# A macaron block on one core: products that clamp, a half-angle arc tangent, norms moved from Pool to ACT, a new order of the mixer, and an earlier routing of the first block

## The reference

```
x = x + 0.5 * moe(layernorm(x))          # "call 0"
x = x + attn(layernorm(x))               # the mixer
x = x + 0.5 * moe(layernorm(x))          # "call 1", the same weights

moe:   shared = (silu(x@sw1) * (x@sw2)) @ sw3
       probs = softmax(x@rw + rb); top 2 of 8 experts, weights renormalised
       routed = sum over the two of w * ((silu(x@ew1[e]) * (x@ew2[e])) @ ew3[e])     # hidden 256

attn:  z, xBC, dt_raw = split(rmsnorm(x) @ in_proj)         # 256, 256+16+16, 4
       u, B, C = split(silu(conv4(xBC))); B = B/(|B|+eps); C = C/(|C|+eps)
       dt = softplus(dt_raw + dt_bias); A = exp(A_log)      # A: 4 heads x 16 states
       step t:  S = 1/(1 + dt^2 A)
                w = S*(w - dt*A*y + dt*B*u);  y = y + dt*w;  o = y . C
       h = x + ((o + D*u) * silu(z)) @ out_proj
       out = h + (silu(rmsnorm(h)@gate) * (rmsnorm(h)@up)) @ down      # hidden 352
```

## Time and profile before

| what | us |
|---|---|
| median of 3 runs | 932.72 (928.23 to 933.27) |
| the profiled execution's own time | 924.96 |
| its span | 923.2 |
| call 0, routing and shared expert | 0 to 131.8 |
| call 0, expert tiles and answers | 131.8 to 275.7 |
| the mixer | 275.7 to 640.8 |
| call 1, routing and shared expert | 640.8 to 764 |
| call 1, expert tiles, then the last combines | 764 to 923.2 |

### The profile page before, as it was taken

The page is one execution under the profiler, slowest core; times in us unless marked ns, Lnnn a source line. Parts: engine busy times, 40 slices in busy tenths (PEclk is TensorE's granted clock), DMA queues, the critical chain, the costliest instruction groups (busy, mean ns, idle before and its releaser), DMA issues. The chain is left out here.

```text
span 923.2 us, 13673 instructions
## 1 busy us (share of the span) xinstructions
PE 666.9 (72%) x3736; PEld 480.5 (52%) x3736; DVE 580.0 (63%) x1762; ACT 351.0 (38%) x592; POOL 597.5 (65%) x744
## 2 busy tenths in 40 slices
PE   2636769899834677959879999797553579988840
PEld 2324447777731255637546575574432347777730
DVE  4714635544527899869996999974724355455427
ACT  1202113444413866646674766411111114444410
POOL 2775653555546899999999998843674732555550
PEclk9966979999985688979998999999586979999985
DMA  7411112222223000000000000000010113222208
GB/s 211 148 53 35 58 50 70 68 78 78 60 77 126 1 1 1 1 0 2 1 1 0 2 1 1 1 1 1 23 56 32 50 55 79 72 72 77 68 27 270
DMA packets 55896, 46.36 MB, mean 50 GB/s; under 512 B 8840, under 2 KB 51437, under 8 KB 55824
## 3 DMA queue, kind: packets, MB, share of 16 engines
q1 hardware_dynamic: 47120, 28.55, 11.0%
q0 software_dynamic: 8704, 16.93, 5.6%
HBM read 25.31 MB, written 21.19 MB: 50 GB/s over the span
## 5 line engine op out<-in xcount | busy, mean ns | idle before, releaser
L718 POOL DMA_INDIRECT ys<-arena,dest x144 | 141.0, 979 | 141.1 <-DVE arena L1449 58.3
L708 POOL DMA_INDIRECT xs<-rows,pos x128 | 124.8, 975 | 65.9 <-issue 36.7
L1912 PE MATMUL ps_go<-w_down_e,arena 128*128 x576 | 78.9, 280 | 19.6 <-DVE arena L1449 19.4
L1912 PEld LDWEIGHTS ps_go<-w_down_e,arena 128*128 128x128 f32 x576 | 69.9, 191 | 25.8 <-issue 25.7
L1449 DVE COPY arena<-ps_go 128x256 f32<-128x256 f32 x72 | 30.6, 425 | 65.6 <-remote 46.3
L942 ACT ACTIVATE silu_a<-ps_a 128x512 f32<-128x512 f32 x32 | 19.0, 597 | 128.2 <-remote 70.0
L1841 PE MATMUL ps_go<-chosen,earlier 128*128 128x32 bf16 x16 | 3.2, 197 | 82.0 <-DVE chosen L1352 70.6
L954 ACT ACTIVATE xt_hi<-ps_tr 128x256 fp32r<-128x256 f32 x72 | 27.4, 384 | 69.6 <-PE ps_tr L1875 44.4
L971 ACT ACTIVATE arena<-ps_go 128x512 f32<-128x512 f32 x72 | 43.1, 598 | 28.1 <-remote 15.3
L1841 PEld LDWEIGHTS ps_go<-chosen,earlier 128*128 128x128 bf16 x16 | 1.6, 100 | 94.2 <-DVE chosen L1352 77.7
L1439 DVE TENSOR_TENSOR hid<-silu_a,ps_a 128x512 f32<-128x512 f32 x36 | 24.7, 687 | 40.8 <-ACT silu_a L962 32.9
(11 more groups left out here) (348 smaller groups left out, 2074.1 us busy)
## 6 DMA issues: line engine op xcount, KB each, us to landing
arena<-xs SPq DMA_DIRECT2D x144, 65.0 KB
rows<-ys SPq DMA_DIRECT2D x8, 512.0 KB, 4.0
...
xs<-rows,pos POOLq DMA_INDIRECT x128
...
```

What stands on the lines that cost most here:

```text
L708: pool.indirect_dma_start(xs, bass.IndirectOffsetOnAxis(pos[:, n, k * TT + t:k * TT + t + 1], 0), rows[:, n * TT + t, :], None).then_inc(s ...
L718: pool.indirect_dma_start(ys, bass.IndirectOffsetOnAxis(dest[:, i:i + 1], 0), y_out[:, p % YRING, j, :], None, bounds_check=2 * TOK - 1, o ...
L1912: r = pe.matmul(ps_k[:, j * P:(j + 1) * P], hid_t[:, p % 2, at:at + P], w_down_e[:, bass.ds(which[2 * p + j], 1), k, :].rearrange("p a d - ...
```

## The change

**Clamps within products.** Before, Pool held the logs of the decays within +-160 (`clamp_c`, `clamp_b`) before ACT took their exponential. Now ACT takes the exponential of the logs as they are, and the two DVE products that use the results take the smaller of the result and 5e34 on the way (`scalar_tensor_tensor` with min and mult, in place of `tensor_tensor` with mult). Both clamps and `theta_max` are gone.

**Half-angle arc tangent.** Before: arctan(min(theta, 1/theta)) plus a correction of -pi/2 where theta > 1 (`theta_side` on Pool, `angle` on DVE), then |.|/(2 pi) on ACT (`to_turns`). Now arctan(theta / (1 + sqrt(1 + theta^2))) is half of the angle, and a Copy with the factor 1/pi gives turns. The root is an Exp (`root`) and the reciprocal a Ln with bias 1 and an Exp. The log log(1 + theta^2) in t3 is kept, and t0 and t3 change roles from `log_sums` on.

**Norms on ACT.** `z_norm` and `h_start` are now ACT activations of Identity with a scale and a bias for each partition, 4 of 128x128 each. `norms` runs three blocks ahead, and amv, arstd, azr and offset have 4 slots in place of 3.

**B and C spread by Pool.** `bc_normed` multiplied and spread B and C in one DVE operation of 128x1024. Now DVE multiplies 128x128 into `bc_nn`, and Pool copies it 8-fold to `bc_rep` (`bc_spread`), for which `bc_features` on PE waits.

**New order** of all four bodies, new PSUM banks in `pb` with the waits that go with them, `combined_block` one block later in its pipeline (at 6, not 7).

**Early routing of block 0.** Pool scatters block 0 before it takes the roots of blocks 2 and 3, and scatters block 1 before those of 4 to 7. DVE in call 0 writes the rows of block 0 before it waits for block 1. The bias `rb` is loaded once for each partition (32 bytes) and broadcast when read. PE's order in the calls is unchanged.

```diff
@@ pool_mixer
-            def z_norm(b, q): ...                                  # 4 x tensor_scalar, to ACT
-            def h_start(b, q): ...                                 # 4 x tensor_scalar, to ACT
-                pool.tensor_scalar(t0[q], t0[q], 1.0, float(-np.pi / 2), ALU.is_gt, ALU.mult).then_inc(theta_side_ready, 1)
-                pool.tensor_scalar(cfs[:, q, :], t5, -CLAMP, None, ALU.max).then_inc(clamps_ready, 1)
-                pool.tensor_scalar(t3[q], t3[q], CLAMP, None, ALU.min).then_inc(clamps_ready, 1)
+            def bc_spread(b, q):
+                n = SQ * b + q
+                pool.wait_ge(bcn_ready, n + 1)
+                after(pool, rep_ps_ready, n)
+                pool.tensor_scalar(bc_rep, bc_nn[:, :, :].rearrange("p g (a n) -> p g a n", a=1).broadcast_to([P, 2 * TT, 2 * NH, DS]),
+                                   1.0, 0.0, ALU.mult, ALU.add).then_inc(bc_rep_ready, 1)
             def body(at):
-                do(c_places, at(-1))
-                do(bc_conv, at(0))
-                do(clamp_c, at(0))
-                do(theta_side, at(0))
-                do(clamp_b, at(0))
                 do(c_relative, at(-1))
                 do(tail, at(-2))
                 do(h_norm, at(-2))
-                do(log_refs, at(0))
                 do(bc_norms, at(0))
                 do(h_add, at(-2))
+                do(log_refs, at(0))
+                do(bc_spread, at(0))
                 do(gated_output, at(-1), 0)
-                do(h_start, at(-1))
-                do(norms, at(2))
-                do(z_norm, at(2))
                 do(gated_output, at(-1), 1)
+                do(bc_conv, at(1))
+                do(norms, at(3))
+                do(c_places, at(0))
@@ pool_ffn
             pool_rstd(pool, own, call * NB + 1)
-            pool_rstd(pool, own, call * NB + 2, 2)
             for n in range(NB):
                 pool_scatter(pool, call * NB + n)
                 if n == 0:
+                    pool_rstd(pool, own, call * NB + 2, 2)
+                if n == 1:
                     pool_rstd(pool, own, call * NB + 4, 4)
@@ act_mixer
+            def z_norm(b, q):
+                    r = act.activation(zn[:, t, :], x_tile(b, q, t), ACT.Identity, bias=offset[:, n % 4, 0, t:t + 1],
+                                       scale=azr[:, n % 4, t:t + 1])                      # 4 of them; h_start alike
+            def root(b, q):
+                act.wait_ge(theta_ready, n + 1)
+                after(act, angle_in_ready, n - 1)
+                own.step(act.activation(t4[q], t3[q], ACT.Exp, scale=0.5))
-                own.step(act.activation(t4[q], t4[q], ACT.Ln))
+                own.step(act.activation(t4[q], t4[q], ACT.Ln, bias=1.0))
-                act.activation(t4[q], t4[q], ACT.Exp, scale=-0.5).then_inc(inv_ready, 1)
+                act.activation(t4[q], t4[q], ACT.Exp, scale=-1.0).then_inc(inv_ready, 1)
-                act.activation(t2[q], t2[q], ACT.Arctan).then_inc(arctan_done, 1)
-                act.wait_ge(angle_ready, n + 1)
-                act.activation(t2[q], t2[q], ACT.Abs, scale=float(1 / (2 * np.pi))).then_inc(turns_ready, 1)
+                step(act.activation(t2[q], t2[q], ACT.Arctan))
+                act.activation(t2[q], t2[q], ACT.Copy, scale=float(1 / np.pi)).then_inc(turns_ready, 1)
@@ tm_copy
                 after(act, o_ps_ready, tile - 1)
+                after(act, ds_ps_ready, tile - 1)
             def body(at):           # the new order of ACT
+                bc_copy 1, softplus_ln 1, z_norm 2, theta 1, root 1, sine_c 0, sine_b 0, silu_u 1 (0, 1), silu_z 1 (0),
+                silu_bc 1, silu_gate -2 (0), zt_copy 2, silu_z 1 (1), silu_gate -2 (1), tm_copy 0 (0), silu_gate -2 (2),
+                inverse_ln 1, inverse_exp 1, tm_copy 0 (1), dt_parts 2, arctan 1, tm_copy 0 (2), softplus_exp 2,
+                tm_copy 0 (3), h_start 0, decays 1, hnt_copy -1
@@ dve_mixer
-                dve.tensor_tensor(bc_rep, bc_tm[...].broadcast_to(shape), bc_n[:, 0, :]...broadcast_to(shape), ALU.mult)
+                dve.tensor_tensor(bc_nn[:, :, :], bc_tm[:, :, :], bc_n[:, 0, :]...broadcast_to([P, 2 * TT, DS]), ALU.mult)
-                dve.tensor_scalar(t4[q], t0[q], 1.0, None, ALU.max).then_inc(theta_max_ready, 1)
-                dve.tensor_tensor(t2[q], t2[q], t4[q], ALU.min).then_inc(angle_in_ready, 1)
-                dve.tensor_tensor(t2[q], t2[q], t0[q], ALU.add).then_inc(angle_ready, 1)
+                dve.tensor_tensor(t2[q], t2[q], t4[q], ALU.mult).then_inc(angle_in_ready, 1)
-                dve.tensor_tensor(t6[q], t6[q], cfs[:, q, :], ALU.mult).then_inc(cf_ready, 1)
+                dve.scalar_tensor_tensor(t6[q], cfs[:, q, :], LARGEST, t6[q], ALU.min, ALU.mult).then_inc(cf_ready, 1)
-                step(dve.tensor_tensor(t0[q], t0[q], t1[q], ALU.mult))
+                step(dve.scalar_tensor_tensor(t3[q], t0[q], LARGEST, t3[q], ALU.min, ALU.mult))
             def body(at):           # the new order of DVE
+                stats_of 5, log_sums 1, c_features 0, b_features 0, b_diagonal 0, b_between 0, mixed -1,
+                ffn_hidden -2 (0, 1), bc_squares 1, combined_block 6, ffn_hidden -2 (2), gram_copy 0 (0),
+                state_update -1 (3), state_update 0 (0), angle_in 1, gram_copy 0 (1), bc_normed 1, gram_copy 0 (2),
+                state_update 0 (1), outputs 0 (0), gram_copy 0 (3), state_update 0 (2), phase_sums 1, sine_args_c 1,
+                outputs 0 (1), dt_sum 2, sine_args_b 1, ffn_add -2
@@ dve_ffn, call 0: stats 0, norm 0, arrived(1), stats 1, route 0, norm 1, places 0, stats 2, 3, route 1, stats 4,
@@                  places 1, stats 5 to 7, norm 2, w_lo 0; then the loop from n = 1.  Call 1: stats 0, 1, norm 0, route 0, ...
@@ pe_mixer
             def body(at):           # the new order of PE
+                outputs 0 (0), state_sum 0 (1), outputs 0 (1), make_gram 0 (3), state_sum 0 (2), token_major 0 (3),
+                h_features -1, outputs 0 (2), project_bc 2, outputs 0 (3), down -2, project_z 2 (1), bc_features 1,
+                project_u 2 (0), project_u 2 (1), project_z 2 (0), z_features 3, out_project 0, gate_up -1 (0),
+                bc_tokens 2, gate_up -1 (1), token_major 1 (0), gate_up -1 (2), make_gram 1 (0), state_sum 0 (3),
+                project_dt 3, state_sum 1 (0), make_gram 1 (1), token_major 1 (1), make_gram 1 (2), token_major 1 (2)
```

422 lines of the change are left out of this document (204 added, 218 removed).

## The result

The changed kernel takes 890.33 us (median of 887.1, 889.51, 891.14 and 895.14) against 932.76 us for the kernel before, run beside it. The ratio is 0.956, 95% interval 0.951 to 0.961: faster by 42 us, where I had forecast 22. The profiled execution took 887.1 us (span 885.1) against 924.96, 37.9 less.

The account below looks back on a forecast made before the run. Pool's lateness was taken to bound the mixer, with PE's 34.45 us a block next. From the 932.72 us median, -19 (mixer) and -3 (calls) gave 911 us; own range 903 to 919, eight in ten 898 to 927.

Parts of the forecast that it names:

- The periods' list: Mixer, six intervals between starts of out_project: each forecast from PE's and DVE's busy time; sum 214.2 us, saving taken as 19.
- The head, "0 with +-4": Mixer before its first full period, 86 us: gains of 2.3 and 1.3 us against up to 3.8 paid; no net change.
- The 3.8 us of loads behind the silus: Mixer's head, ACT: two table loads and two activations behind the four silus would cost up to 3.8 us.
- Pool, "no bound, with 7 us to spare": Mixer: Pool falls from 36.2 to 27.6 us a block, so it no longer bounds the period.
- DVE "2.9 under PE's content": Mixer: DVE falls from 34.4 to 31.6 us a block, 2.9 us below PE's own work.
- PE is the next bound: Mixer: with Pool relieved, a full block's period falls to PE's own 34.45 us at full clock and no further.
- PE has room: Rival, mixer: PE's busy time is overstated and the period falls to 32.5 us; total 892 us, chance 0.08.
- Relief, 11.7 us of Pool's work: Mixer: z_norm, h_start, two clamps and theta_side leave Pool, together 11.7 us a block.
- The calls, -3: First stage of both calls: scatter queue 4.7 us earlier in call 0, 2.0 later in call 1; together -3 us.
- From profile to median: Whole kernel: the 22 us saving was taken from the runs' median, 932.72 us, 7.8 above the profiled execution.
- `bc_spread` held up DVE: Rival, mixer: Pool's spread stalls DVE's products, making the period 0.8 us longer than forecast; total 916 us, chance 0.08.
- The stops in call 0: Rival, calls: denser scatters keep PE, ACT and DVE stopped once or twice more, 20.5 us each; 932 or 952, chance 0.10.

Follow-up runs that it names:

- combine_7: The changed kernel with the combines of call 0's results one body earlier, as before the change: mixer 337.4 us, ratio 0.958 to the kernel before.
- norms_act_old: The kernel before with only its two norms moved from Pool to ACT, old order kept: mixer 348.0 us, ratio 0.978 to the kernel before.
- pool_plus: The changed kernel with Pool's spread of B and C carried out three times in a row: mixer 342.7 us, ratio 0.963 to the kernel before.

## Why the prediction was wrong

The direction was right, and of the mechanism the wait: PE's wait for the gated output went, and the full periods fell to PE's content and a bit. The size was off, 911 against 890.3, and so was what I said of slack. The 20.7 us between them, by the steps of the prediction:

- *The periods' list, "each the larger of PE's busy time and DVE's less 3": 8.4 us too long, 6.1 of them in the sixth interval.* This is the step that failed. I gave each interval the work that it had held in the earlier trace rows. But the new order sets half of `project_u`, half of `project_z` and `z_features` ahead of the `out_project` that they stood just behind. (The offsets in the bodies, 1 before and 2 now, overstate this: that of `out_project` itself went from -1 to 0.) So ten records of PE, 4.9 us, left the sixth interval, and as many stand in the head, where PE had 33 us of idle time. With them DVE's `log_sums` (3.4 us) and Pool's `bc_conv` (6.4) left the sixth interval. What holds that interval is DVE and not PE: DVE was busy for 34.20 of 35.20 us and is for 25.89 of 26.88, where my rule left it 31.2. I followed one steady block and never its first and last. The list also breaks its own rule twice: the third interval should have been at least 36.95 by DVE's 39.95, and I took 35.5; the sixth at most 32.5, and I took 33.0. The fourth interval is 1.8 shorter than my number, by the clock of 1.00 that I had named and not taken.
- *The head, "0 with +-4": measured -4.3.* The earlier statistics gave 2.2 to 3.1 (`combine_7`) where I had 2.3, and the norm on ACT gave 2.6 in the old order (`norms_act_old`) where I had 1.3. The 3.8 us of loads behind the silus, which were to take this back, don't show, and 13 more records of PE fit in.
- *Pool, "no bound, with 7 us to spare", and DVE "2.9 under PE's content": the idle time is there, the freedom to use it isn't, and a second mistake hid this.* The busy times of the third and fourth interval came out near the forecast (27 and 32 us), and Pool idles 6 us in one piece. But 2.1 us more of Pool cost 1.6 an interval, by DVE's scan and copy that stood still beside Pool's product, and 1.9 more of DVE cost 0.5 and 0.8. `bc_spread` was mis-sized the other way, 1.06 us and not 3.1, below my lower bound of 1.7. With the price that I gave it the mixer would have been 8 to 9 us longer. Two errors cancelled in part, which is luck.
- *PE is the next bound:* right, but as one of four. 34.20 us is its content, the changed kernel's intervals are 35.0, and nearly any addition on any engine shows. The rival "PE has room" is out: the sixth interval is short for want of work. In the fifth PE is busy for 33.77 of 33.77 us with its weight loads at 22.57, as in the earlier trace rows.
- *Relief, 11.7 us of Pool's work:* the two norms, 6.6 of it, did it all in the old order. I had spread the credit over four edits.
- *The calls, -3: measured -6.7 in the profiles.* The queue's start was right: first scatter forecast at 18.4, measured 17.34, and 18.83 where the data of block 1 still came late, as I had assumed; third batch forecast at 44.1, measured 43.38. I put no price on the bias's smaller load; by itself it is worth 6.6 us, but here it only backs up the new order. In call 1 the third batch came 2.0 us later, as forecast, but the stage didn't follow it: it took 118.7 to 119.9 us with the old order (six profiles) and 116.0 to 119.1 with the new (fourteen).
- *From profile to median:* the kernel before was profiled 7.8 us under its median, the kernel after 3.2. That is 4.6 us of the miss, beside 12.4 in the mixer and 3.7 in the calls. The step from profile to median was taken from one kernel's runs; that it came out smaller here is chance, as far as the runs show.

The ranges were too narrow for this: own range 903 to 919, eight in ten 898 to 927. The rival that came nearest, 892, was for another reason. I allowed for each cost by itself, and for nothing that a new order does at both ends of a pipeline. Of the other rivals, `bc_spread` held up DVE by 0.5 us in two of eight blocks (L1208, 1.10 and 0.96 us in place of 0.5); DVE's slow place is beside `gated_output`. With `bc_spread` at 3.1 us (`pool_plus`) Pool did hold up DVE, by 1.7 us in the third interval and by way of `gated_output`. The stops in call 0 split up: in place of one of 20.52 us stand 8.86, 7.56 and 10.26, and PE's idle time in the first 120 us went only from 54 to 52 us.
